# Two score steps of an attention loop change places: the 256-column step before the two-piece step

## The reference, cut to what matters

```
q, k, v = xn @ wq + bq, xn @ wk + bk, xn @ wv + bv      # 16 heads of 64
scores = einsum('bhqd,bhkd->bhqk', q, k) / sqrt(64)
scores = where(tril(ones, k=-1), -inf, scores)          # a query sees keys at or after it
a = softmax(scores, axis=-1)
h = einsum('bhqk,bhkd->bhqd', a, v)
out = h @ w0 + b0 + residual
```

## Time and profile before

| | |
|---|---|
| median of 3 runs | 1018.42 us (1016.66 to 1019.63) |
| the profiled execution's own time | 1017.03 us |
| its span in the trace | 1015.3 us |
| PE busy | 940.3 us, 93% of the span |
| DVE, ACT, POOL busy | 63%, 53%, 70% |
| mean granted clock of PE | 0.973 of full speed |

### The profile page before, as it was taken

The page is one execution under the profiler, slowest core; times in us unless marked ns, Lnnn a source line. Parts: engine busy times, 40 slices in busy tenths (PEclk is TensorE's granted clock), DMA queues, the critical chain, the costliest instruction groups (busy, mean ns, idle before and its releaser), DMA issues.

```text
span 1015.3 us, 20139 instructions
## 1 busy us (share of the span) xinstructions
PE 940.3 (93%) x7525; PEld 598.3 (59%) x7525; DVE 636.5 (63%) x1904; ACT 539.7 (53%) x737; POOL 707.4 (70%) x521
## 2 busy tenths in 40 slices
PE   3699999999999998999999999999999999999962
PEld 2466666666666565665665665566666666566542
DVE  4656566556657768556667767656666665756354
ACT  5135556554445565665455565666456456465443
POOL 7237767786666768876577877776588776776752
PEclk9689999999999999999999999999999999999985
DMA  4000001011100100101000211100101211000101
GB/s 112 2 21 11 14 23 23 23 23 43 23 23 3 42 23 23 23 22 43 13 13 23 64 23 23 22 23 2 43 23 23 65 23 22 22 4 22 24 22 41
DMA packets 61808, 26.92 MB, mean 27 GB/s; under 512 B 39056, under 2 KB 53776, under 8 KB 61712
## 3 DMA queue, kind: packets, MB, share of 16 engines
q1 hardware_dynamic: 61712, 25.64, 10.8%
HBM read 22.76 MB, written 2.35 MB: 25 GB/s over the span
## 4 chain that ended last, share of the span: by engine, by line
PE 73%; POOL 11%; DVE 6%; ACT 5%; issue 3%; DMA 0%; POOLq 0%; ACTq 0%
PE po L667 21%; PE st L652 15%; POOL total L438 9%; PE sc L618 8%; PE st L706 5%; PE st L647 5%; PE st L584 4%; ACT ring L888 3%; PE sc L677 3%; PE st L586 3%; PE st L585 3%; PE st L600 2%; DVE sc L1056 2%; PE st L601 1%; PE st L602 1%
## 5 line engine op out<-in xcount | busy, mean ns | idle before, releaser
L438 POOL TENSOR_TENSOR total<-total,ring 128x1024 f32<-128x1024 f32 (+1 forms) x315 | 543.7, 1726 | 253.2 <-PE po L667 210.1
L1056 DVE CUSTOM_DVE_ANT_0 sc<-sc,key_mask 128x512 f32<-128x512 f32 (+1 forms) x496 | 230.4, 522 | 146.6 <-PE sc L618 144.3
L888 ACT ACTIVATE ring<-st 128x1024 f32<-128x1024 f32 (+1 forms) x256 | 228.9, 918 | 164.5 <-PE st L652 146.4
L1059 DVE TENSOR_REDUCE least<-sc 128x1 f32<-128x512 f32 x268 | 170.3, 678 | 75.6 <-PE sc L618 71.1
L667 PE MATMUL po<-ring,v_sb 128*64 128x512 f32 (+3 forms) x1280 | 210.7, 467 | 0.0
L652 PE MATMUL st<-q_high,k_low 64*128 64x512 f32 (+3 forms) x768 | 177.9, 449 | 0.0
L667 PEld LDWEIGHTS po<-ring,v_sb 128*64 128x64 f32 x1280 | 86.7, 137 | 128.4 <-issue 123.3
L618 PE MATMUL sc<-k_high,q_high 64*128 64x512 f32 (+3 forms) x768 | 138.1, 389 | 17.9 <-DVE least L1059 6.5
L652 PE MATMUL st<-q_low,k_high 64*128 64x512 f32 (+3 forms) x768 | 137.5, 343 | 0.0
L652 PE MATMUL st<-q_high,k_high 64*128 64x512 f32 (+3 forms) x768 | 137.0, 343 | 0.0
L618 PEld LDWEIGHTS sc<-k_high,q_high 64*128 64x128 f32 x768 | 70.3, 189 | 86.6 <-issue 62.9
(11 more groups left out here) (157 smaller groups left out, 1240.4 us busy)
## 6 DMA issues: line engine op xcount, KB each, us to landing
inv_row<-sums_dram SPq DMA_DIRECT2D x62, 256.0 KB, 4.0
x_a<-x SPq DMA_DIRECT2D x4, 512.0 KB, 4.9
sums<-sums_row SPq DMA_DIRECT2D x124, 2.0 KB, 2.1
x_b<-x SPq DMA_DIRECT2D x3, 512.0 KB, 5.8
out<-res_b SPq DMA_DIRECT2D x3, 512.0 KB, 4.8
ring<-w_pairs SPq DMA_DIRECT2D x1, 1152.0 KB, 6.8
shift_row<-shift_t SPq DMA_DIRECT2D x64, 4.0 KB
x_a<-x SPq DMA_DIRECT2D x2, 256.0 KB, 3.3
```

Of the source, the lines that this page charges most:

```text
L438: nc.gpsimd.tensor_tensor(so_far, so_far, tile_of(n, s)[:, :, col:col + w], ALU.add).then_inc(s_add, 1)
L888: nc.scalar.activation(tile_of(n, s)[:, :, 0:w], st[s % 2][:, :, 0:w], ACT.Exp, scale=SCALE).then_inc(s_exp, 1)
L1056: last = nc.vector.tensor_tensor_reduce(bank[:, col:col + w], bank[:, col:col + w], key_mask[:, 0:w], -1.0, 3e38, ALU.add, ALU.min, least[ ...
L1059: last = nc.vector.tensor_reduce(least[:, h, a:a + 1], bank[:, col:col + w], AX.X, ALU.max, negate=True)
```

## The change

In `TILES` the second and the third entry of the third stretch change places:

```diff
     TILES = [[(0, 7, 512, 0)], [(0, 6, 512, 0)], [(0, 5, 512, 0)],
              [(0, 1, 256, 0)], [(0, 4, 512, 0)], [(0, 3, 512, 0)], [(0, 2, 384, 0), (0, 0, 128, 384)],
-             [(1, 7, 512, 0)], [(1, 6, 384, 0), (1, 4, 128, 384)], [(1, 5, 256, 0)]]
+             [(1, 7, 512, 0)], [(1, 5, 256, 0)], [(1, 6, 384, 0), (1, 4, 128, 384)]]
     STEPS = len(TILES)
     T_STEPS = [range(0, 3), range(3, 7), range(7, 10)]
```

## The result

| | before | changed |
|---|---|---|
| median | 1018.26 us | 1021.88 us |
| lowest to highest of 12 runs each | 1014.94 to 1019.64 | 1019.37 to 1022.90 |
| ratio, 95% interval | | 1.0038 (1.0026 to 1.0050) |
| profiled execution, its span | 1017.03, 1015.3 | 1022.72, 1021.0 |

The changed kernel is slower by 3.6 us; the interval of the ratio reaches from 2.6 to 5.1 us, so it excludes that nothing changed, but its lower end is the forecast's 2.6. That forecast came with a range up to 1024.2. The two profiled spans differ by more, 5.7 us, and 1.0 of that lies ahead of the loop: exp 0 of slot 0 starts 58.2 us into the trace before and 59.2 in the changed one. Over all the traces of this study it starts between 56.6 and 59.7, whatever the kernel, so spans of single executions can't be compared to better than that; distances within a slot can.

What follows compares the result with a forecast made beforehand. PE was taken to set the pace (73% of the span). 20 ordinary slots 0.8, two late 0.5, slot 30 0.8, slot 31 0.5 sum to +2.6 us: 1021.0 us, +0.26%, range 1016.8 to 1024.2.

Steps and rivals of the forecast that it cites:

- Where it happens: L600's wait for exponentials goes; L647's for `total` goes from 30 times to near 60, gaining some 10 us.
- v fill gain: Start of the v fill behind the turn: it no longer waits for exp 8, 0.26 us gained in an ordinary slot.
- Rival one: Turn to v fill: fill waits for the turn's matmul to end, gains only 0.19; +4.2 us, 1022.6, slower; chance 0.22.
- the strict form of the rule of the Trainium skill: At turn and v fill: weight loads overlap a running matmul only on different row groups; sum would be 4.2 us.
- T9's loss: T9, now long, waits for exp 7 and ends 1.26 behind it, not 0.96: 0.30 us lost in an ordinary slot.
- ordinary slot: Slot where T7 is not late; net +0.04 us each, bounds -0.06 to +0.14, counted in 20 slots as 0.8 us.
- late one: Slots 9, 11, 17, 19, T7 late behind DVE: 0.52 lost against 0.26, +0.26 us each; two counted, 0.5.
- Slots 30 and 31: Last slots, without v fill: +0.80 us as L714 waits for a full exp 9; +0.5 us from a longer T9.
- The eight slots: Slots whose next sum waits for POOL, not PE: 11, 19 and six ordinary ones; delay up to that wait is swallowed.
- Rival two: At T9: it finds exp 7 done, so only the gain is left; -3.9 us, 1014.5, faster; chance 0.12.
- rival three: The two stalls only change places, the last slots' 1.3 us lost in spread; 1018.4, at most 1019.7; chance 0.12.
- Rival four: Turn's DMA before T0: its 0.4 us cover gives way, T0 waits 0.1 in 30 slots; 1024.0; chance 0.04.

Runs made afterwards that it cites:

- the third experiment: The changed kernel with T9's two pieces exchanged, 128 columns first and 384 last; ratio 1.0040 to the kernel before, 1020.76 us.
- the exchange in T6: The kernel before with T6's two pieces in the other order, 128 columns first and 384 last; ratio 0.9989, 1016.64 us.
- both halves of the change: Two kernels, the kernel before with the change in units 0 to 29 alone (1.0016) and in units 30 and 31 alone (1.0015).
- a run of their own: The kernel before with the change in units 3, 11, 15, 16, 19, 23, 24 and 27 alone; ratio 0.9997, 1017.45 us.

## Why the prediction was right, and by how much it was off

- **Where it happens**: as forecast. The wait of L600 went, that of L647 came in 29 more slots. It was to bring some 10 us and brought 12.1.
- **v fill gain**: 0.26, exactly (turn to v fill 0.42 to 0.16). Rival one, the turn holding the fill to its end, would have been 0.23 and falls, and with it the strict form of the rule of the Trainium skill (TensorE: Matmul & The Clock Gate, Part 3: Packing small matmuls — row/col tiling) that I had weighed: the fill's load at 516.87 starts 0.07 before the turn's modelled end, with all rows in use by both. Inside the v fill the overlap is wider: the load of L601 starts at 516.98, 0.11 behind the start of L600's product, which is on all rows too and lasts to 517.26.
- **T9's loss**: the mis-sized term. I had 0.30 and it is 0.35. T9's own end is right (1.26 behind exp 7); the step that failed is "the S, the turn and the v fill move with it". S starts 0.16 before T9's end, not 0.19 as the products of 256 columns let it, and needs 0.38 to the turn instead of 0.35. Net 0.09 in an ordinary slot instead of 0.04, still inside my bounds, and 0.30 instead of 0.26 in a late one. That it belongs to the 128-column products is what the third experiment and the exchange in T6 show: the 0.05 from S to the next product went with them, and came back inside the step. How the loads and products share it I did not separate. The prediction took T6's end as the price of T9 and the distances behind it from the narrow T9; T6's own S and the product behind it, in the same trace, give 0.05 + 1.42 = 1.47 to the turn, which is what was measured.
- **Slots 30 and 31**: +0.78 and +0.51, forecast +0.80 and +0.5.
- **The eight slots**: confirmed by a run of their own.
- **Sum**: 20 x 0.09 + 2 x 0.30 + 0.78 + 0.51 = 3.7 us; measured 3.6, and 3.3 the second time. Mine was 2.6. The intervals, 2.6 to 5.1 us and 2.1 to 4.6, would allow either sum; it is the distances in the slots that decide for 3.7. So the outcome lay across the 0.3% line that I drew at 3.06 us, and 0.46 for within against 0.42 for slower was the wrong way round by the 1 us of that term.
- **Rival two** (T9 finds exp 7 done) and **rival three** (even) fall: T9 waits in every slot, and both halves of the change are slower by themselves (1.0016 and 1.0015, both intervals above 1). **Rival four** falls: T0 waits for nothing. The turn's copy is 2.23 behind exp 7, 0.37 later than before. The forecast of 0.47 let it wait for the end of exp 9, while in both traces it starts 0.1 ahead of that end.

## What to carry to other kernels

When a wait is removed by reordering, look for the wait that the other half of the swap creates, and measure both from the same event: here 0.26 us given back against 0.35 spent in an ordinary slot and 0.56 in a late one. A small net effect per slot must be sized with the shapes of the instructions at the seam, since 0.05 us in 20 slots is 1 us: take the price of a step from start to start of what follows it, in a place where the same shapes meet, and not to its own end. And a wait of the bounding engine can be filled with work of that engine that is ready there, where no other engine waits for what then comes later: the weighing put ahead of the v fill, except where a fill feeds ACT and DVE, gave 0.9979, 2.1 us less than before and less than either order of steps. Even there only 0.11 of the 0.26 in a slot came back, since the split of the weighing cost the rest.

## What the runs showed of the hardware

- PE starts 0.05 to 0.06 us behind the end of the exponential that it waits for, in T9 (515.23 to 515.29) and in L714 (953.74 to 953.79) alike.
- A score step that ends in 128-column products costs PE some 0.05 us more, up to the product behind the next S, than its modelled end and the distances behind a step of 256 columns let one expect; with the small piece ahead of the wide one the same cost stands inside the step (step to S 1.10 instead of 1.04, S to the next product 0.33 instead of 0.38, in T9 and T6 alike).
- A run of products of one shape that is cut in two cost more here: 1.01 us instead of 0.91 for the same weighing, and 1.51 instead of 1.46 for the rest.
- The weight load of a product on all 128 rows runs while another product on all 128 rows is under way (L601's load from 516.98 to 517.17, L600 from 516.87 to 517.26).
- An operation of DVE on four columns takes 0.16 us by itself. When it runs into one of POOL's operations it ends 0.02 to 0.04 behind that one's end, so that it took 0.32 to 2.33 us, 191 times in the fourteen traces; in one of them that cost the kernel 2.7 us.
